# Applies of the two near key tiles as three passes of halves, with a new order of each head's work

## The reference

```python
x = x @ ws[0]; for w in ws[1:]: x = silu(x) @ w        # memory MLP, two layers
grads = vmap(grad(chunk_loss))(mem_ws, keys, lr, values)
momentum = assoc_scan(mom_gate, -grads); updates = assoc_scan(1 - decay, momentum)
x = q @ (mem_w0 + updates[0])
vals = silu(x) @ (mem_w1 + updates[1])
vals = rmsnorm(vals) * (mh_gamma + 1) * gate;  out = vals @ w_combine
```

## Time and profile before

| | us |
|---|---|
| median of 3 runs | 1191.07 (1189.88 to 1191.84) |
| the profiled execution | 1189.44 |
| its span, first to last instruction | 1187.6 |
| mean granted TensorE clock | 0.965 of full speed |
| head stage | about 181 to 1183 |

### The profile page before, as it was taken

One profiled execution on the slowest core, in us unless ns is written; L12 is line 12 of the kernel. 1 busy time (PEld: TensorE's weight loads), 2 busy tenths in 40 slices (PEclk: granted clock), 3 DMA queues, 4 the chain that ended last, 5 costly groups with the idle time before them and its releaser, 6 DMA issues. The chain is left out here.

```text
span 1187.6 us, 20255 instructions
## 1 busy us (share of the span) xinstructions
PE 1100.7 (93%) x6649; PEld 917.9 (77%) x6650; DVE 720.1 (61%) x1892; ACT 679.8 (57%) x1369; POOL 561.9 (47%) x571
## 2 busy tenths in 40 slices
PE   4589869999999999999999899998999899999995
PEld 3356547788888888888888788887888788888884
DVE  4488856877655655655555455554555555556785
ACT  4666635566565565655555455554556455556663
POOL 3167753487764434444433343343434343344553
...
DMA packets 57537, 40.32 MB, mean 34 GB/s; under 512 B 4595, under 2 KB 52061, under 8 KB 57310
## 3 DMA queue, kind: packets, MB, share of 16 engines
...
...
## 5 line engine op out<-in xcount | busy, mean ns | idle before, releaser
L1105 DVE TENSOR_TENSOR p_sb<-bank,cf 128x512 f32<-128x512 f32 (+3 forms) x512 | 218.9, 483 | 1.1 <-PE bank L828 1.0
L1286 POOL TENSOR_TENSOR sq_rest<-sq,sq_high 128x450 f32<-128x450 f32 x64 | 67.2, 1050 | 247.1 <-ACT sq_high L995 247.1
L851 PE MATMUL bank<-p_sb,du_t 128*128 128x450 f32 (+3 forms) x512 | 131.1, 399 | 0.0
L851 PE MATMUL bank<-p_sb,err_t 128*128 128x450 f32 (+3 forms) x512 | 130.1, 397 | 0.0
L851 PEld LDWEIGHTS bank<-p_sb,err_t 128*128 128x128 f32 x512 | 85.0, 190 | 40.0 <-DVE p_sb L1105 16.9
L851 PEld LDWEIGHTS bank<-p_sb,du_t 128*128 128x128 f32 x512 | 82.0, 190 | 43.8 <-issue 29.8
L1138 DVE SCALAR_TENSOR_TENSOR acc<-bank,rg,acc 128x128 f32<-128x128 f32 x224 | 62.9, 344 | 84.6 <-POOL rg L1274 84.6
L1290 POOL TENSOR_TENSOR sq_low<-sq_rest,sq_mid 128x450 bf16<-128x450 f32 x64 | 66.6, 1041 | 100.1 <-ACT sq_mid L1012 99.9
L973 ACT ACTIVATE s_sb<-bank 128x512 f32<-128x512 f32 x64 | 38.3, 599 | 108.0 <-PE bank L828 108.0
L967 ACT ACTIVATE xs<-bank 128x450 f32<-128x450 f32 x64 | 35.1, 548 | 109.7 <-PE bank L851 108.5
L1174 DVE SCALAR_TENSOR_TENSOR du<-q_sb,bank 128x512 f32<-128x512 f32 x64 | 44.0, 688 | 87.5 <-PE bank L828 87.5
...
## 6 DMA issues: line engine op xcount, KB each, us to landing
...
```

Of the source, the lines that this page charges most:

```text
L851: last = pe.matmul(out[:, P * i:QW], rows[:, i, :], p_sb[:, P_COL[i]:P_COL[i] + QW - P * i], start=False, stop=True, skip_group_check=True)
L1105: last = nc.vector.tensor_tensor(dst, src, w, ALU.mult)
L1286: nc.gpsimd.tensor_tensor(sq_rest[:], sq[:], sq_3[0][:], ALU.subtract).then_inc(g_rest, 1)
```

## The change

Tiles 0 and 1 (`NEAR`) of both applies become three passes of halves; tiles 2 and 3 (`FAR`) stay plain. For this the weighed scores of the near tiles are split into `p_2`: the high half is copied by ScalarE (`whole`), the low one subtracted by GpSimd for the second layer and by VectorE (`rest`) for the first. The transposed error and du are split in the same way (two copies on ScalarE, `turned_rest` on VectorE). The order of the step is new on TensorE, ScalarE and VectorE: near second scores, the product of s and the one of xs stand together, the far scores, transposes and far apply follow, then ffn1, then the near apply with the product into U and the near first scores; ffn2 and the output product come before w_x and the apply in XB. xf is made later on VectorE. To make room, du shares memory with th, sq with err, sq_rest with xs, and three small tables of the routing with the expert weights, whose load (SyncE) moves behind the waits on `v_shifted` and `v_coef`. The core of the diff, with 16 blanks taken off in front of the lines inside `attend`'s blocks:

```diff
-SC_BANK = [4, 5, 6, 5]
-SC_COL = [0, 0, 0, 384]
-P_COL = [0, 512, 1024, 896]
-SC_ORDER = [0, 1, 3, 2]
+SC_BANK = [4, 5, 6, 6]
+SC_COL = [0, 0, 0, 256]
+P_COL = [0, 512, 896, 1152]
+NEAR, FAR = (0, 1), (2, 3)
...
 P_COLS = sum(S - P * i for i in range(T))
+PART_COL = [0, QW]
+PART_COLS = 2 * QW - P
...
-        err_t = sb("err_t", [P, T, D])
-        du = sb("du", [P, S])
-        du_t = sb("du_t", [P, T, D])
-        p_sb = sb("p_sb", [P, P_COLS])
+        err_t, err_2t = sb("err_t", [P, 2, D]), pair("err_2t", [P, 2, D])
+        du = th
+        du_t, du_2t = sb("du_t", [P, 2, D]), pair("du_2t", [P, 2, D])
+        p_sb, p_2 = sb("p_sb", [P, P_COLS]), pair("p_2", [P, PART_COLS])
...
     return product(out[:, 0:width], [part[:, at[1], :] for part in w], y, stop=stop)
-def scores(left_2, right_2, left, right, done, tiles=SC_ORDER):
+def scores(left_2, right_2, left, right, done, tiles):
...
         out = m.bank[SC_BANK[i]][:, SC_COL[i]:SC_COL[i] + QW - P * i]
-        if i < 2:
+        if i in NEAR:
...
             last = pe.matmul(out, left[:, (i - 2) * P:(i - 1) * P], right[:, P * i:], start=True, stop=True)
-        if i != 1:
+        if i != 2:
             last.then_inc(done, 1)
-def apply(out, rows, made, n):
-    for i in SC_ORDER:
-        if i != 3:
-            pe.wait_ge(made, SC_BANKS * n + {0: 1, 1: 2, 2: 3}[i])
-        last = pe.matmul(out[:, P * i:QW], rows[:, i, :], p_sb[:, P_COL[i]:P_COL[i] + QW - P * i],
+def apply_near(out, rows_2, whole, low, n):
+    for i in NEAR:
+        pe.wait_ge(whole, 2 * n + i + 1)
+        pe.wait_ge(low, 2 * n + i + 1)
+        cols = slice(PART_COL[i], PART_COL[i] + QW - P * i)
+        for j, (u, v) in enumerate(((0, 0), (0, 1), (1, 0))):
+            last = pe.matmul(out[:, P * i:QW], rows_2[u][:, i, :], p_2[v][:, cols], start=False, stop=True, skip_group_check=True)
+    return last
+def apply_far(out, rows, made, n):
+    pe.wait_ge(made, SC_BANKS * (n + 1))
+    for i in FAR:
+        last = pe.matmul(out[:, P * i:QW], rows[:, i - 2, :], p_sb[:, P_COL[i]:P_COL[i] + QW - P * i],
...
         pe.wait_ge(a_dt, n)
+        pe.wait_ge(v_dtl, n)
...
         pe.wait_ge(v_p0, SC_BANKS * (k + 1))
-        scores(s_2[s[1] % 2], xs_2, s_sb[s[1] % 2][:, 2 * P:], xs, p_s1)
+        scores(s_2[s[1] % 2], xs_2, s_sb[s[1] % 2][:, 2 * P:], xs, p_s1, NEAR)
+    if f is not None:
+        pe.wait_ge(g_sl, n + 1)
+        product(EB[:], [w[:] for w in w1], [part[:] for part in s_2[h % 2]], start=False).then_inc(p_e, 1)
+    if s is not None:
+        pe.wait_ge(v_acc, k)
+        product(VB[:, 0:QW], [w[:] for w in w1], [part[:] for part in xs_2])
+        scores(s_2[s[1] % 2], xs_2, s_sb[s[1] % 2][:, 2 * P:], xs, p_s1, FAR)
...
         pe.wait_ge(m.s_rows[r], 16 * (turn(s) + 1))
-        pe.wait_ge(a_xs, k + 1)
-        pe.transpose(XB[:, 0:P], m.rows[r][:, 0:D], m.ident[:]).then_inc(p_t, 1)
-    if f is not None:
-        pe.wait_ge(g_sl, n + 1)
-        product(EB[:], [w[:] for w in w1], [part[:] for part in s_2[h % 2]], start=False).then_inc(p_e, 1)
-    if s is not None:
-        pe.wait_ge(v_acc, k)
-        pe.wait_ge(a_et, k + 1)
-        product(VB[:, 0:QW], [w[:] for w in w1], [part[:] for part in xs_2])
-        apply(VB, err_t, v_p1, k).then_inc(p_v, 1)
-    if x is not None:
-        pe.wait_ge(v_xf, x + 1)
         pe.wait_ge(a_qa, n + 1)
-        for k4 in range(FB):
-            last = pe.matmul(QA[:, k4 * P:k4 * P + P], w1s[:, k4 * P:k4 * P + P], xf, start=True, stop=True)
-        last.then_inc(p_h, 1)
+        pe.transpose(QA[:, 0:P], m.rows[r][:, 0:D], m.ident[:]).then_inc(p_t, 1)
...
         last.then_inc(p_et, 1)
+    if s is not None:
+        pe.wait_ge(a_et, k + 1)
+        apply_far(VB, err_t, v_p1, k)
+    if x is not None:
+        pe.wait_ge(v_xf, x + 1)
+        for k4 in range(FB):
+            last = pe.matmul(QA[:, k4 * P:k4 * P + P], w1s[:, k4 * P:k4 * P + P], xf, start=True, stop=True)
+        last.then_inc(p_h, 1)
+    if s is not None:
+        pe.wait_ge(v_etl, k + 1)
+        apply_near(VB, err_2t, a_p1, g_p1, k).then_inc(p_v, 1)
+    if f is not None:
...
         pe.wait_ge(v_p1, SC_BANKS * n)
-        scores(yk, qa_2, yb, qa, p_s0, SC_ORDER[:-1])
+        scores(yk, qa_2, yb, qa, p_s0, NEAR + FAR)
...
         last.then_inc(p_dt, 1)
-        scores(yk, qa_2, yb, qa, p_s0, SC_ORDER[-1:])
-        pe.wait_ge(a_et, n + 1)
-        project(XB, m.w_x, f, SHIFT)
-        pe.wait_ge(a_dt, n + 1)
-        apply(XB, du_t, v_p0, n).then_inc(p_x, 1)
...
             pe.matmul(VB[0:r, t * P:t * P + P], vals[:, t * P:t * P + r], m.w_out[:, s[1], :], start=True, stop=True)
+    if f is not None:
+        pe.wait_ge(a_et, n + 1)
+        pe.wait_ge(v_etl, n + 1)
+        project(XB, m.w_x, f, SHIFT)
+        pe.wait_ge(a_dt, n + 1)
+        pe.wait_ge(v_dtl, n + 1)
+        apply_near(XB, du_2t, a_p0, v_p0l, n)
+        apply_far(XB, du_t, v_p0, n).then_inc(p_x, 1)
+    if s is not None:
...
             def _(act):
+def whole(i, made, done, n):
+    act.wait_ge(made, SC_BANKS * n + i + 1)
...
         act.wait_ge(p_x, k + 1)
+        act.wait_ge(g_lo, k)
...
         nc.scalar.copy(qa[:], QA[:, 0:QW]).then_inc(a_qa, 1)
+    if s is not None:
+        whole(0, v_p1, a_p1, k)
+    if f is not None:
...
         nc.scalar.copy(err[:], EB[:]).then_inc(a_err, 1)
+    if s is not None:
+        whole(1, v_p1, a_p1, k)
+    if f is not None:
...
         nc.scalar.copy(vals[:], VB[:, 0:QW]).then_inc(a_v, 1)
+    if f is not None:
+        act.wait_ge(p_et, n + 1)
+        nc.scalar.copy(err_2t[0][:].rearrange("p t d -> p (t d)"), XB[:, 0:2 * P])
+        nc.scalar.copy(err_t[:].rearrange("p t d -> p (t d)"), XB[:, 2 * P:]).then_inc(a_et, 1)
+    if s is not None:
         act.wait_ge(a_v, k + 1)
+        act.wait_ge(v_el, k + 2 if f is not None else k + 1)
...
         nc.scalar.copy(sq_3[0][:], sq[:]).then_inc(a_hi, 1)
-    if f is not None:
-        act.wait_ge(p_et, n + 1)
-        nc.scalar.copy(err_t[:].rearrange("p t d -> p (t d)"), XB[:]).then_inc(a_et, 1)
...
     if f is not None:
+        whole(0, v_p0, a_p0, n)
+        whole(1, v_p0, a_p0, n)
         act.wait_ge(p_dt, n + 1)
-        nc.scalar.copy(du_t[:].rearrange("p t d -> p (t d)"), EB[:]).then_inc(a_dt, 1)
+        nc.scalar.copy(du_2t[0][:].rearrange("p t d -> p (t d)"), EB[:, 0:2 * P])
+        nc.scalar.copy(du_t[:].rearrange("p t d -> p (t d)"), EB[:, 2 * P:]).then_inc(a_dt, 1)
...
         nc.scalar.copy(sq_3[1][:], sq_rest[:]).then_inc(a_mid, 1)
+    if f is None and s is None:
+        gate_rows(B - 1)
...
+def weigh(h, made, done, n, tiles):
+    for i in tiles:
...
         w = cf[:, h, i * NC + 2 * i:i * NC + NC].unsqueeze(2).broadcast_to([P, ch, C])
-        if i != 3:
-            dve.wait_ge(made, SC_BANKS * n + {0: 1, 1: 2, 2: 3}[i])
+        dve.wait_ge(made, SC_BANKS * n + min(i + 1, SC_BANKS))
         last = nc.vector.tensor_tensor(dst, src, w, ALU.mult)
-        if i != 1:
+        if i != 2:
             last.then_inc(done, 1)
+def rest(i, whole, done, n):
+    dve.wait_ge(whole, 2 * n + i + 1)
+    cols = slice(PART_COL[i], PART_COL[i] + QW - P * i)
+    nc.vector.tensor_tensor(p_2[1][:, cols], p_sb[:, P_COL[i]:P_COL[i] + QW - P * i], p_2[0][:, cols], ALU.subtract).then_inc(done, 1)
+def turned_rest(parts, bank, whole, done, n):
+    dve.wait_ge(whole, n + 1)
+    nc.vector.tensor_tensor(parts[1][:].rearrange("p t d -> p (t d)"), bank[:, 0:2 * P],
+                            parts[0][:].rearrange("p t d -> p (t d)"), ALU.subtract).then_inc(done, 1)
...
         nc.vector.tensor_copy(ids[r][:], m.rows[r][:, D:ROW].bitcast(I32)).then_inc(v_ids, 1)
-        dve.wait_ge(v_w, x + 1)
-        dve.wait_ge(p_t, x + 1)
-        nc.vector.tensor_scalar(xf, XB[:, 0:P], w1s[:, PAR:PAR + 1], w1s[:, PAR + 1:PAR + 2], ALU.mult, ALU.add).then_inc(v_xf, 1)
...
         dve.wait_ge(p_x, k + 1)
-        weigh(s[1], p_s1, v_p1, k)
+        weigh(s[1], p_s1, v_p1, k, NEAR)
...
             nc.vector.tensor_tensor(yb[:], high[:, 2 * P:], low[:, 2 * P:], ALU.add).then_inc(v_y, 1)
+        dve.wait_ge(a_th, n + 1)
+        dve.wait_ge(a_s, n + 1)
+        nc.vector.scalar_tensor_tensor(q_sb[:], U[:], 1.0, s_sb[h % 2][:], ALU.add, ALU.subtract).then_inc(v_q, 1)
+    if s is not None:
+        weigh(s[1], p_s1, v_p1, k, FAR)
+    if f is not None:
...
             nc.vector.tensor_copy(cf[:], m.coef[:, bass.ts(f[0], 1), :, :].rearrange("p a h c -> p (a h) c")).then_inc(v_cf, 1)
-        dve.wait_ge(a_th, n + 1)
-        dve.wait_ge(a_s, n + 1)
-        nc.vector.scalar_tensor_tensor(q_sb[:], U[:], 1.0, s_sb[h % 2][:], ALU.add, ALU.subtract).then_inc(v_q, 1)
...
         nc.vector.scalar_tensor_tensor(q_sb[:], th[:], 1.0, q_sb[:], ALU.add, ALU.mult).then_inc(v_g, 1)
+    if x is not None:
+        dve.wait_ge(v_w, x + 1)
+        dve.wait_ge(p_t, x + 1)
+        nc.vector.tensor_scalar(xf, QA[:, 0:P], w1s[:, PAR:PAR + 1], w1s[:, PAR + 1:PAR + 2], ALU.mult, ALU.add).then_inc(v_xf, 1)
```

(19 more changed lines are left out.)

20 lines of the change are left out of this document (9 added, 11 removed).

## The result

| | before | changed |
|---|---|---|
| median, us | 1191.45 (1189.88 to 1193.96) | 1330.22 (1329.17 to 1334.15) |
| ratio | | 1.1159, 95% interval 1.1134 to 1.1184 |
| span, us | 1187.6 | 1328.9 |
| mean granted clock | 0.965 | 0.952 |

What follows compares the result with a forecast made beforehand. TensorE was taken as the bound. Block heads +1.64 x 40 = 66, plain heads +0.77 x 24 = 18, plus 8, 5 and 1 gave +98 on 1189.4, median 1288 us; 8-in-10 range 1232 to 1310.

Steps and rivals of the forecast that it cites:

- TensorE's saving: Both applies per head: halves' passes save 0.65 us, four runs becoming three save 0.10; together -0.75 us per head.
- Wait 1, s_low: TensorE's product of s and w1, moved right behind the near scores, waits 0.50 us for s_low in every head.
- Wait 2, the far weights: apply_far waits for VectorE's far weights of p: 0.31 us in a block head, 0.42 in a plain one.
- Wait 3, xf: In block heads ffn1 waits 0.47 us for xf, which VectorE now makes behind the second q_sb.
- Wait 4, the relu: In block heads ffn2 waits 0.78 us for ScalarE's relu, which stands behind vals, err_t copies, sq and sq_high.
- Wait 5, the engines' mutual hold-up: VectorE against GpSimd: q_sb held, +0.33 us per block head; err_low or qa_low late, +0.50 per plain head.
- Rival (c): VectorE yields to GpSimd for whole instructions: 0.7 us more in 24 plain heads, 1305 us; chance 0.10.
- Batch 0 and last batch: VectorE's longer tails: +5 us estimated for two heads of batch 0; last batch +1.2 in each of 7 heads, 8.
- Rival (e): The halves' passes save nothing, since started singly behind waits they cost what plain ones did: +48, 1336 us; chance 0.03.
- (b): Some wait thought open is hidden, the relu's first: 31 us less, 1257 us; chance 0.12.
- (a): VectorE and GpSimd don't hold each other up: 25 us less, 1263 us; chance 0.15.
- (d): TensorE stays the bound and only s_low's wait is left: -0.25 us per head, 1175 us; chance 0.10.

Runs made afterwards that it cites:

- The edit that removes it: Changed kernel with all four tiles of the second scores together again, ahead of the product of s and w1: 1285.31 us, ratio 1.0756.
- the two experiments on them: Each near apply as one plain product, low half of the rows left out: 1354.82 us on the changed kernel, 1240.46 us on the 1227.01 us repaired kernel.
- the mended kernels: Changed kernel with far scores, relu, routing and xf moved, err_low and q_sb reading PSUM: 1229.22 us; with sq_low later 1228.99; then XB's far tiles first 1227.01.
- three attempts: Changed kernel with all repairs together, 1229.22 us; on top of it GpSimd's sq_low behind p_low, 1228.99; on top of that far tiles first in XB, 1227.01.

## Why the prediction was partly wrong, step by step

**TensorE's saving.** The direction was right, the size wrong: 0.75 was forecast, 0.48 came in block heads and about 0.2 in plain ones. The rate within a run held (six passes take 517.65 - 516.60 = 1.05 us, forecast 1.06). The plain tiles did not: they cost 1.30 us, not the 1.40 that the prediction got by taking the scores' 0.52 off the apply of 1.92, so the two applies save 0.48 and not 0.65. "Four runs become three" did not hold either. A wait inside a run ends it, and the pass behind it is longer again: 379.25 to 379.59 is 0.34, and 510.57 to 510.80, without a wait, is 0.23. A block head has four starts as before (501.15, 504.80, 509.42, 515.91). A plain one has seven, three more than before (behind the waits at 379.25, 383.93 and 385.23; 0.11, 0.08 and 0.08 us).

**Wait 1, s_low.** Right: forecast 0.50; the product starts 0.48 later than it could (504.17 + 0.15 to 504.80), in plain heads 0.49 (373.25 + 0.15 to 373.89).

**Wait 2, the far weights.** Right in kind, a little small: 0.42 against 0.31 in a block head (transposes end at 507.26), 0.53 against 0.42 in a plain one. The edit that removes it gave the largest single gain, because it closes wait 1 as well (TensorE's waits for s_low fall from 23.7 to 3.2 us in all); the prediction had listed both without saying that one order causes them.

**Wait 3, xf.** 0.33 against 0.47 (the far apply takes 0.50, from 507.68 to 508.18; ffn1 starts at 508.51).

**Wait 4, the relu.** 0.85 against 0.78 (513.26 to 514.11), and 0.65 came back when the relu was moved. Right.

**Wait 5, the engines' mutual hold-up.** This is the step that failed, and the saving above is the other one. In a block head the 0.33 wasn't there: q_sb started at 507.45, when p_low was 0.13 us from its end and 0.09 us ahead of qa_low, and took 0.68 us, where the prediction had named 0.69 as a sign of being wrong (in the block heads of batches 3 to 6 it took 0.68 to 1.19, mostly 0.72). So the block head's +1.64 was right to 0.04 by luck, because two errors cancel: waits 1 to 4 sum to 2.08 instead of 2.06, the lock is 0 instead of 0.33, the saving 0.48 instead of 0.75. By rows that makes 2.08 - 0.48 = 1.60, and 1.60 was measured. In plain heads the term was priced as 0.50, one operation late for one product. In truth it strikes twice, and each time at an operand of TensorE. The forms are q_sb or err_low beside p_low and qa_low, and p_low of tile 1 beside sq_low. These rows are of the head of 16.33 us, but for the one at 409.41, which is of one of 15.92:

```profile
376.56 2.04 DVE L1217 SCALAR_TENSOR_TENSOR q_sb<-thu,q_sb 128x512 f32<-128x512 f32 x1
...
383.74 1.34 DVE L1150 TENSOR_TENSOR p_low<-p_sb,p_high 128x322 fp32r<-128x322 f32 x1
...
409.41 1.64 DVE L1224 TENSOR_TENSOR err_low<-err,err_high 128x512 fp32r<-128x512 f32 x1
```
```profile
375.07 1.87 POOL L1342 TENSOR_TENSOR p_low<-p_sb,p_high 128x450 fp32r<-128x450 f32 x2
376.89 1.15 POOL L1319 TENSOR_TENSOR qa_low<-qa,qa_high 128x450 fp32r<-128x450 f32 x1
...
383.70 1.03 POOL L1355 TENSOR_TENSOR sq_low<-xs,sq_mid 128x450 bf16<-128x450 f32 x1 [0.59 <-ACT sq_mid L1051]
```

In the head of 16.33 us q_sb is held until qa_low ends, 2.04 us instead of 0.68, and err_low behind it is 0.77 late for the product. Four of the 24 plain heads are of this kind. In sixteen others, as in one of 15.92 us (the row at 409.41), q_sb comes first, qa_low waits for it (1.60 us from 408.90), and err_low is the one that is held, 1.63 to 1.65 us; in the head shown it is 0.37 late for the product. The second meeting, of p_low and sq_low, costs 0.62 at 385.23. Du's low half isn't held, it only comes late at the end of VectorE's longer list, by 0.37 where the prediction had 0.10. By the plain head's own rows: waits of 0.49 + 0.53 + 0.77 + 0.37 + 0.62 = 2.78, less the saving of 0.48 and plus the three starts (0.27), give +2.57; measured +2.61. The forecast was +0.77. Of the difference some 1.26 are waits and 0.54 the saving; with +2.2 in the heads of 15.92 us it makes, over 24 heads, most of the missing time. One of these waits, p_low's, the prediction had never looked for: it walked the block head to its end and took the plain one as the same with less. As I read it, the plain head is the harder one, because it has no ffn1 and ffn2 that give the other engines time.

Rival (c), from the Trainium skill (SBUF — State Buffer, "Who interferes with whom"), that two SBUF inputs on VectorE and a GpSimd operation exclude each other for a whole instruction, was the right mechanism at a tenth of the chance, and it was priced at one place only (1305). The rows agree in this: q_sb ends 0.56 us after qa_low does (378.60 and 378.04), err_low from PSUM isn't held at all, and p_low and sq_low, started within 0.04 us of each other, take 1.38 us together, where sq_low alone takes 1.04 and p_low 0.48 on average once sq_low waits for it. With the order of issue they don't always agree: q_sb at 376.56 met p_low, which ended at 376.94, and qa_low, which started at 376.89, went ahead of it. The other three heads with a q_sb of 2.03 us or more look the same.

**Batch 0 and last batch.** The +5 was an estimate without rows, and it fell short by the most: about 10 us lie in the sixth head alone (27.03 against 16.81 in the kernel before). The new order on TensorE puts the wait on VectorE's routing result in front of the output product and the apply. The prediction had looked at the routing on VectorE and SyncE, not at what TensorE has queued behind it. In the last batch the lateness of VectorE was forecast at 1.2 us in each of seven heads, 8 in all; it measured 1.1 in four distances and 1.4 in one, 5.7 in all, so that term was right in kind and somewhat large. The rest of batch 7's 21.3 is the plain head. Before the first and after the last head 10.4 us came where 1 was forecast; no run tests these.

**Rival (e)**, that the passes save nothing, is ruled out by the two experiments on them; (b), that the relu's wait is hidden, by the wait itself; (a), that the engines don't hold each other up, was right of q_sb in block heads and wrong in plain ones; (d), that TensorE stays the bound, holds for the block heads of the mended kernels alone (15.53 to 15.57). No version run here beats the kernel before. What stays open is whether an order exists in which plain heads also keep 13.7 us: three attempts moved the loss from one late operand to the next (14.60, 14.29, 14.25) without removing it.
